# Causal mask of the score maxima: mask matmuls against a masked minimum on VectorE, in an attention and expert block

## What is computed

```python
xn = _layernorm(x, axis=-1)
q, k = _rope(xn @ Wq.T, xn @ Wk.T)               # 16 heads of 8
scores = jnp.einsum('bqhd,bkhd->bhqk', q, k) * scale
causal = jnp.triu(jnp.ones((S, S), dtype=bool), k=1)
scores = jnp.where(causal, -jnp.inf, scores)
attn = jax.nn.softmax(scores, axis=-1)
out = jnp.einsum('bhqk,bkhd->bqhd', attn, v).reshape(B, S, H * Dh)
x = x + out @ Wo.T + ffn(xn)                     # top 2 of 8 experts, 128 -> 512 -> 128
```

## Time and profile before

| what | value |
|---|---|
| median of 3 runs | 774.55 us (770.61 to 775.82) |
| the profiled execution's own time | 773.38 us |
| its span in the profile | 771.6 us |
| TensorE's mean granted clock | 0.958 of full speed |

### The profile page before, as it was taken

One profiled execution on the slowest core, in us unless ns is written; L12 is line 12 of the kernel. 1 busy time (PEld: TensorE's weight loads), 2 busy tenths in 40 slices (PEclk: granted clock), 3 DMA queues, 4 the chain that ended last, 5 costly groups with the idle time before them and its releaser, 6 DMA issues. The chain is left out here.

```text
span 771.6 us, 19063 instructions
## 1 busy us (share of the span) xinstructions
PE 715.4 (93%) x6544; PEld 420.0 (54%) x6544; DVE 574.9 (75%) x977; ACT 457.2 (59%) x1090; POOL 255.5 (33%) x306
## 2 busy tenths in 40 slices
PE   9899898999999999999999997999999989989897
PEld 3465343544544544544444445999999934343344
DVE  6956988788788788788788784666666659878344
ACT  3544025667677677676676675666666637647451
POOL 2566111523433423333324331000000057556651
PEclk9899999999999999999999998999999979979599
DMA  8599840337356235135144041322222361211644
GB/s 219 136 226 236 259 63 16 54 67 123 79 87 131 58 62 79 34 56 77 29 64 73 23 73 53 96 68 68 68 67 68 88 113 42 54 32 41 155 124 135
DMA packets 64623, 69.40 MB, mean 90 GB/s; under 512 B 9934, under 2 KB 52430, under 8 KB 64490
## 3 DMA queue, kind: packets, MB, share of 16 engines
q1 hardware_dynamic: 60458, 60.08, 35.5%
q0 software_dynamic: 4096, 8.40, 4.2%
HBM read 41.11 MB, written 26.67 MB: 88 GB/s over the span
## 5 line engine op out<-in xcount | busy, mean ns | idle before, releaser
L737 ACT ACTIVATE probs<-bank 128x512 f32<-128x512 f32 (+3 forms) x768 | 326.1, 492 | 209.3 <-PE bank L1223 202.9
L845 DVE TENSOR_REDUCE mx<-bank 128x2 f32<-128x1024 f32 (+3 forms) x320 | 348.1, 1115 | 84.4 <-PE bank L1206 67.6
L1223 PE MATMUL bank<-stack 64*128 64x512 f32 (+3 forms) x768 | 210.5, 445 | 18.9 <-ACT probs L737 18.3
L637 POOL TENSOR_SCALAR_AFFINE_SELECT probs<-probs 128x512 f32<-128x512 f32 x128 | 81.8, 640 | 432.3 <-ACT probs L737 276.9
L1257 PE MATMUL bank<-probs,vst 128*32 128x256 f32 (+3 forms) x2304 | 193.9, 410 | 5.2 <-POOL probs L637 2.9
L1223 PEld LDWEIGHTS bank<-stack 64*128 64x128 f32 x768 | 94.0, 190 | 181.6 <-ACT probs L737 135.7
L1199 PE MATMUL bank<-stack 64*128 64x512 f32 (+3 forms) x768 | 163.6, 384 | 4.4 <-DVE mx L845 4.4
L1199 PEld LDWEIGHTS bank<-stack 64*128 64x128 f32 x768 | 83.7, 192 | 13.7 <-DVE mx L845 11.1
L1301 PE MATMUL bank<-tiles_s,staged 128*128 128x128 f32 x576 | 79.6, 282 | 0.7 <-ACT tiles_s L742 0.7
L1257 PEld LDWEIGHTS bank<-probs,vst 128*32 128x32 f32 x2304 | 46.4, 110 | 58.9 <-ACT probs L737 19.4
L1319 PE MATMUL bank<-staged,q_high 128*128 128x128 f32 x576 | 76.6, 276 | 0.5 <-DVE k_high L1027 0.5
(11 more groups left out here) (131 smaller groups left out, 447.5 us busy)
## 6 DMA issues: line engine op xcount, KB each, us to landing
stack<-parts_d SPq DMA_DIRECT2D x96, 128.0 KB
slots_in_d<-const_s SPq DMA_DIRECT2D x4, 1152.0 KB, 9.0
tiles_s<-slots_in_d SPq DMA_DIRECT2D x72, 64.0 KB, 1.8
slots_out_d<-k_high SPq DMA_DIRECT2D x72, 64.0 KB, 1.6
early<-in_w_experts SPq DMA_DIRECT2D x8, 514.0 KB, 5.3
stack<-parts_d SPq DMA_DIRECT2D x64, 64.0 KB
parts_d<-probs SPq DMA_DIRECT2D x8, 512.0 KB, 6.1
heads_d<-xnT SPq DMA_DIRECT2D x124, 18.0 KB
```

Source lines behind the costliest of these rows:

```text
L637: pool.affine_select(out=t, in_=t, compare_op=ALU.is_ge, fill=0.0, base=0, pattern=[[0, HG], [1, P]], channel_multiplier=-1).then_inc(s["d ...
L737: nc.scalar.activation(probs[n % 3][:, h, q0:HALF], st_of(at)[:, 0:HALF - q0], ACT.Exp, scale=SCALE).then_inc(s["probs_made"], 1)
L845: v.tensor_reduce(to, src.rearrange("p g (a k) -> p g a k", k=w), AX_X, ALU.max, negate=True).then_inc(s["scores_read"], 1)
L1223: mm(st_of(at)[:, 0:HALF - q0], kstk[r][g][:, hp, kb * P:(kb + 1) * P], qstk[r][g][:, hp, c * HALF + q0:(c + 1) * HALF], start=True, stop=True
```

## The change

Items 4 to 11 of units 1 to 15 (`hides`) get no mask matmuls. In their place VectorE adds a constant tile while it reduces: `later_s`, 512 wide in bf16, is 0 but for −1e30 past the diagonal of its last 128 columns, and its last w columns line up with an item of width w. In place of one reduction over both heads there is one `tensor_tensor_reduce` per head: the sum of scores and mask, times −1, reduced by the minimum, which is the negated maximum. Its elementwise result goes in bf16 into `hidden_scores`, four parts of `q_high`, which two following items use in turn; a wait on VectorE's own earlier reads keeps them apart. GpSimd makes `later_s` after it has split the projections. Unit 0, items 0 to 3 and items 12 to 19 stay as they were.

```diff
--- before.py
+++ after.py
@@ -191,6 +191,7 @@
         before_b = sb("before_b", [P, P], BF16)
         ones_b = sb("ones_b", [P, P], BF16)
         chosen_b = rt2[3].bitcast(BF16)[:, 0:NT * E]
+        later_s = sb("later_s", [P, HALF], BF16)
         eps_s = sb("eps_s", [P, 1])
         table_s = sb("table_s", [P, 2])
         stacks = [sb(f"stack{i}", [P, 2, PAIRS, S], F32R) for i in range(4)]
@@ -215,6 +216,8 @@
         zero_rows, one_rows = (mrow[i][0:2, :].unsqueeze(1).broadcast_to([2, PAIRS * T, P]) for i in range(2))
         gT = tiles_s[:, 6:8, :]
 
+        hidden_scores = [q_high[:].bitcast(BF16)[:, g * HALF:(g + 1) * HALF] for g in range(4)]
+
         xt = [tiles_s[:, i, :] for i in range(4)]
         xtT = [tiles_s[:, 4 + i, :] for i in range(2)]
         w_s = [staged[:, i, :] for i in range(2)]
@@ -239,7 +242,7 @@
 
         names = """const_loaded w_loaded tab_loaded eps_ready table_loaded consts_ready pool_step
         ln_halves ln_stats ln_std ln_rstd xn_ready xnT_made xnT_ready
-        q_made qs_made k_made ks_made q_used qs_used k_used ks_used roped ones_ready rows_zero rows_ready
+        q_made qs_made k_made ks_made q_used qs_used k_used ks_used roped ones_ready rows_zero rows_ready later_cleared later_ready
         q_first k_first q_split k_split stack_cleared zeros_stored masks_loaded v_made v_copied logits_made logits_copied """
 
         names += """rt_step rt_shifted rt_exped chosen_ready counted gT_made gT_kept routed
@@ -319,6 +322,11 @@
         COMBINES = [[0, 0, 1, 0, 1, 2, 3, 3, 2, 1, 1, 1], [0, 1, 1, 0, 2, 2, 3, 3, 2, 1, 1, 1],
                     [0, 1, 1, 0, 2, 3, 3, 3, 2, 1, 1, 1], [1, 1, 1, 0, 1, 2, 2, 2, 2, 1, 1, 0]]
         assert sum(map(sum, TRANSFERS)) == sum(map(sum, COMBINES)) == 2 * NT
+
+        def hides(u, n):
+
+            subs = ITEMS[n][1]
+            return u > 0 and len(subs) == 1 and subs[0][0] // CK == subs[0][1]
 
         def share_of(table, r, i):
 
@@ -602,6 +610,11 @@
             pool.sem_inc(s["consts_ready"], 1)
             for b in range(B):
                 split(b)
+            pool.memset(later_s[:], 0.0).then_inc(s["later_cleared"], 1)
+            pool.wait_ge(s["later_cleared"], 1)
+            pool.affine_select(out=later_s[:, HALF - P:HALF], in_=later_s[:, HALF - P:HALF], compare_op=ALU.is_ge,
+                               fill=-1e30, base=0, pattern=[[-1, P]], channel_multiplier=1
+                               ).then_inc(s["later_ready"], 1)
             pool.wait_ge(s["k_split"], B)
             pool.memset(b2_blk, 0.0).then_inc(s["b2_zeroed"], 1)
 
@@ -840,6 +853,17 @@
                 qb, c, a = subs[0]
                 w = piece_width(qb, c)
                 dve.wait_ge(s["scores_made"], u * MI + n + 1)
+                if hides(u, n):
+                    if hides(u, n - 2) or u > 1:
+                        earlier_read = u * MI + n - 2 if hides(u, n - 2) else (u - 1) * MI + n + 6
+                        dve.wait_ge(s["scores_read"], earlier_read + 1)
+                    for g in range(2):
+                        last = v.tensor_tensor_reduce(
+                            hidden_scores[n % 2 * 2 + g][:, 0:w], ms[(r * MI + n) % 2][:, g * HALF:g * HALF + w],
+                            later_s[:, HALF - w:HALF], -1.0, 3e38, ALU.add, ALU.min,
+                            mx[r % 2][:, 2 * hp + g, a, qb % CK:qb % CK + 1])
+                    last.then_inc(s["scores_read"], 1)
+                    return
                 src = ms[(r * MI + n) % 2].rearrange("p (g k) -> p g k", g=2)[:, :, 0:len(subs) * w]
                 to = mx[r % 2][:, 2 * hp:2 * hp + 2, a:a + len(subs), qb % CK]
                 v.tensor_reduce(to, src.rearrange("p g (a k) -> p g a k", k=w), AX_X, ALU.max, negate=True
@@ -1089,6 +1113,8 @@
             step(v.tensor_scalar(expert[:], ends, float(E - 1), None, ALU.min))
             dve.sem_inc(s["routed"], 1)
 
+            dve.wait_ge(parts_written[0][0], 16 * PARTS * 2)
+            dve.wait_ge(s["later_ready"], 1)
             for n in range(AT_START):
                 read_item(1, 1, n)
             all_units(dve, unit, None, experts)
@@ -1193,7 +1219,7 @@
                     pe.wait_ge(s["scores_read"], u * MI + n - 1)
                 for i, (qb, c, _) in enumerate(subs):
                     w = piece_width(qb, c)
-                    diagonal = qb // CK == c
+                    diagonal = qb // CK == c and not hides(u, n)
                     for g in range(2):
                         col = g * HALF + i * w
                         last = mm(at[:, col:col + w], qstk[r][g][:, hp, qb * P:(qb + 1) * P],
```

## The result

Over 15 executions of each kernel, on several chips, the changed kernel took 778.79 us (median, 772.58 to 785.47) and the kernel before 773.62 (767.04 to 778.26). The ratio is 1.0093, with a 95% interval of 1.0058 to 1.0127: slower by about 7 us, inside the stated range of 776 to 818, but under half of the 16.3 us of the forecast. Ratios and intervals here go by the faster of two states that executions of a kernel can fall into, so they differ from the quotient of the medians, which is 1.0067 in this case. The profiled execution took 775.28 us, its span is 773.5 us.

The account below looks back on a forecast made before the run. VectorE was taken to bound one gapless stretch of about 7.5 us per period. Eleven groups adding 9.8 us, unit 1's items 1.5 and units 13 to 15 5.0 gave 16.3 on 773.4: 790 us, range 776 to 818.

Parts of the forecast that it names:

- The price of a pair: VectorE's masked minimum plus accumulator read, per head of a 512 wide item: 0.72 us, so an item 1.44 against 1.13.
- The sum: Per period, items 8 to 11 add 1.24 us, 0.35 comes back from an earlier start; with other units 16.3 us in all.
- lower bound: Least cost of a masked minimum with its accumulator read on VectorE: 0.665 us, +0.20 us an item.
- The main part: The masked minimum itself on VectorE, 512 wide from PSUM: 0.53 us of elements and 0.06 fixed, 0.60 us.
- the read: VectorE's second instruction on one element, reading the accumulator out after each masked minimum: taken as 0.12 us.
- rival 2: TensorE wins: VectorE's items cost nothing more, the time falls by up to 5 us to 768 us; chance 0.11.
- rival 1: The pair drains: VectorE's accumulator read waits for the main part's end, 0.84 us a pair, 818 us; chance 0.24.
- The stretch: About 7.5 us per period, items 8 to 13 and the heads' copy, where VectorE never idles; longer items add 1.24 us.
- The masks' worth: Fewer mask matmuls on TensorE (items 4 to 8) let item 8 start 0.35 us sooner each period.
- Rival 5: The clock: the longer stretch lets TensorE's granted clock fall in the periods, 1 to 2 us more each, 805 us; chance 0.07.
- Units 0 and 13 to 15: Longer reads of unit 1's items, within unit 0, add 1.5 us; units 13 to 15, beside gathered combines, 5.0 us.
- signs of being wrong: Period at most 29.5 us, pair under 0.6 or over 0.85, clock under 1.00 in periods, or difference outside units 0 to 14.

Follow-up runs that it names:

- e4: Changed kernel with only the 512 wide items (8 to 11) masked by VectorE, the 384 wide ones by TensorE as before: 780.4 us, ratio 1.0104 to before.
- e5: Changed kernel with only the 384 wide items (4 to 7) masked by VectorE, the 512 wide ones by TensorE as before: 772.1 us, ratio 0.9990.
- e1: Changed kernel with TensorE's mask matmuls put back, so both engines mask items 4 to 11: 777.2 us, ratio 1.0068 to before.
- e2: Changed kernel without VectorE's masking: neither engine masks items 4 to 11 of units 1 to 15, VectorE reduces as before: 767.8 us, ratio 0.9959.
- e12: The changed kernel run again, unaltered, beside the kernel before on the same chip: 777.0 us, ratio 1.0038.
- e6: Changed kernel with VectorE masking only from unit 2 on, unit 1's items masked by TensorE as before: 778.6 us, ratio 1.0024.
- e10: Changed kernel plus two idle matmuls per unit where TensorE waits for the joined maxima: 773.0 us, ratio 1.0037 to before.
- e14: Repeat of the kernel before plus two idle matmuls per unit, beside fresh runs of before: 767.0 us, ratio 0.9905.
- e9: Changed kernel with TensorE also keeping the mask matmuls of items 8 to 11, so these are masked twice: 779.2 us, ratio 1.0104 to before.
- e11: Kernel before plus two idle matmuls per unit where TensorE waits for the joined maxima: 770.1 us, ratio 0.9870.
- e8: Kernel before with one item moved from step 2 to step 11, ahead of another copy: 793.7 us, ratio 1.0256.

## Why the prediction was right and wrong

**The price of a pair: wrong, the step that failed.** The sum took 0.72 us for a masked minimum and its read, so +0.31 us an item, with a lower bound of 0.665. Measured are 0.61, so +0.09 us an item; with it the same sum gives 4 x 0.09 − 0.35 = 0.01 us a period and nothing for the other units, in place of 16.3 us. The main part, taken at 0.60, was right to 0.01; the read costs no time of its own, as it starts with the next instruction. The lower bound was no bound: it took from small instructions in a row that each adds at least its gap. The +0.09 us lie at the very point (0.09) that rival 2 named as where it decides. That rival, at 0.11, was what happened to the periods: shorter by 0.17 us. A main part's row is 0.69 us long and the next starts after 0.61, so rival 1 is out. The sentence of the Trainium skill that it was set beside (VectorE: DVE Perf Modes, "The DRAIN you can't avoid": the next operation waits for an empty pipe) is not borne out by these rows; the same section adds that a next operation that is not held starts earlier, which the prediction left out, and with that the trace agrees.

**The stretch: right.** The longer items add to it one for one, 7.84 against 7.48 us, and TensorE waits at its end. e4 and e5 show it from both sides: with the 512 wide items the period grew by 0.13 us, with the 384 wide ones outside the stretch it fell by 0.31. Together they give −0.18, the −0.17 of the changed kernel. In e1, where the masks stay, 0.23 of the 0.36 us reached the period.

**The masks' worth: roughly right.** 0.35 us a period in the sum, and item 8 does start 0.41 us sooner; e2 has 0.54 for the whole period, and the difference of the changed kernel and e1 is 0.40. e1 and e2 add up to +0.23 − 0.54 = −0.31 a period, the changed kernel has −0.17; the parts are not independent.

**The clock: wrongly left out of the likeliest case.** Rival 5 had it with a chance of 0.07, as an extra on top of longer periods. By the comparison at equal clock it was all of the loss. The median clock fell by 0.012 (e12 against before on its chip) to 0.019 (the first comparison, against 0.958 of all executions of before), which at 5.9 us for 0.01 is 7 to 11 us, against 2.6 us gained at full clock: 4 to 9 us, where 0.38% to 0.93%, 3 to 7 us, were measured. The profile of before had the warning (0.72 in 677 to 695), and the spread of the three times shown, 770.61 to 775.82, was as large as the effect of 0.01 of clock.

**Units 0 and 13 to 15.** The 1.5 and 5.0 us forecast were built on the same price. Unit 0 was 1.2 us longer in the profile with a clock of 0.86; e6 could not tell whether that is systematic, and the kernel before with idle matmuls had a clock of 0.82 and 38.8 us there in both its profiles. Of the last distance between joining steps, with combines beside it, two profiles at full clock can be compared: 31.14 us in e10 and 30.53 in e14, both with idle matmuls. That is 0.6 us longer in the changed kernel, where the forecast had 1.7 us a unit.

**Direction.** Slower was right, for a reason that carried 7% of the chances. Had the price been known, the same sum would have said no change. That the time rose at all is luck as far as the forecast's mechanism goes. Two of the prediction's own signs of being wrong did come: a period under 29.5 us, and a granted clock under 1.00 in a period.

**Open.** Why the clock falls in the changed kernel and in e9, but not in e1, is not settled. Idle matmuls raised it in e10, e11 and e14 and fewer masks together with longer reads lowered it, but no share that was read from the rows orders all the kernels.

## What to carry to other kernels

A change that takes work off TensorE can lose more in granted clock than it gains in its stages: compare the granted clock of many executions, and the length of a stage at full clock, as two separate numbers. Idle matmuls in a wait that is there anyway left the full-clock period as it was and gave 0.4 to 1.3% here in the kernel before. Before an item is moved away from one gate (a copy that other work waits for), look what stands behind it at the next: e8's wait moved and about doubled, from 0.37 to 0.68 us.

## What was not expected of the hardware

The read of VectorE's accumulator (83 ns long) starts together with the next instruction, so that a masked minimum with a read takes 0.61 us for 512 elements from PSUM and 0.48 us for 384 (326.80 to 327.28 in the changed kernel): the elements at 0.96 a ns and some 0.08 us. A granted clock lower by 0.01, which is 1.04% of 0.958, goes with 5.9 us of 773 (0.76%). Taking mask matmuls away and making reads longer moved the clock by 0.0065 (e2) and 0.001 (e1) against before on the same chip; together they moved it by 0.012 to 0.019.
